# First route: all rows kept in SBUF, normalised by ScalarE in the scaling rounds and the selection

## The reference, cut to what matters

```
x = x + 0.5 * ffn(layernorm(x)); x = x + mixer(layernorm(x)); x = x + 0.5 * ffn(layernorm(x))

def ffn(x):                                   # x is normalised
    logits = x @ gate_w                       # (8, 2048, 8 experts)
    t = log(clip(logits, 1e-6))
    for _ in range(8):                        # Sinkhorn: over the tokens, then over the experts
        t = t - logsumexp(t, tokens); t = t - logsumexp(t, experts)
    vals, idx = top_k(exp(t) per expert, 256) # 256 tokens for each expert
    routed_back[idx] = (x[idx] @ experts[e]) * vals     # where experts share a token, the last stands
```

## Time and profile before

| | us |
|---|---|
| median of 3 runs (lowest, highest) | 3546.92 (3545.2, 3549.64) |
| the profiled execution | 3556.01 |
| its span, first to last instruction | 3554.5 |

### The profile page before, as it was taken

How to read it: one execution, slowest core, us unless ns; L and a number is a source line. 1 busy time by engine, 2 the same in 40 slices (tenths; PEclk the granted TensorE clock), 3 DMA queues, 4 the chain that set the end, 5 groups by cost and what they waited for, 6 DMA issues and landing times. The chain is left out here.

```text
span 3554.5 us, 29882 instructions
## 1 busy us (share of the span) xinstructions
PE 2753.7 (77%) x9684; PEld 1514.2 (43%) x9684; DVE 3150.0 (89%) x2664; ACT 2099.4 (59%) x2219; POOL 1295.2 (36%) x871
## 2 busy tenths in 40 slices
PE   6303778899889889988988998898789677874555
PEld 4202333354346335434634543463345255433444
DVE  7996489999999999999999999999999968994555
ACT  6101568876877787687778768677866634221111
POOL 0003254437244443724444372444011110016665
PEclk8556899999899999989999998999899887885777
DMA  8103377788778778877877887787677669233342
GB/s 332 66 0 108 84 171 177 153 180 182 154 172 164 177 153 179 183 153 172 163 177 155 180 183 151 173 163 174 127 145 139 130 122 364 89 158 117 131 143 89
DMA packets 128024, 553.85 MB, mean 156 GB/s; under 512 B 19782, under 2 KB 55272, under 8 KB 79424
## 3 DMA queue, kind: packets, MB, share of 16 engines
q0 software_dynamic: 75168, 393.49, 53.1%
q1 hardware_dynamic: 52736, 158.94, 12.1%
HBM read 152.62 MB, written 117.45 MB: 76 GB/s over the span
## 5 line engine op out<-in xcount | busy, mean ns | idle before, releaser
L1312 DVE TENSOR_TENSOR_SCAN state<-state,drive 128x2048 f32<-128x2048 f32 x512 | 2223.7, 4404 | 51.0 <-ACT state L1518 50.9
L1518 ACT ACTIVATE state<-delta,neg_a 128x2048 f32<-128x2048 f32 x512 | 1018.8, 2005 | 216.8 <-DMA delta<-xc 84.0
L1769 PE MATMUL ps_states<-state,ident 128*128 128x512 f32 x1792 | 854.3, 622 | 78.7 <-DMA state<-state 64.3
L1193 POOL DMA_DIRECT2D state<-state x255 | 233.5, 916 | 1310.1 <-DVE state L1312 1286.4
L1671 PE MATMUL ps_proj<-x1t,w_in 128*128 128x512 f32 x1024 | 514.5, 648 | 84.7 <-ACT xc L1467 29.8
L1769 PEld LDWEIGHTS ps_states<-state,ident 128*128 128x128 f32 x1792 | 349.1, 201 | 482.0 <-issue 384.8
L1687 PE MATMUL ps_proj<-conv_in,tap 128*128 128x512 f32 x1024 | 488.7, 629 | 54.5 <-ACT conv_in L1431 33.9
L1122 POOL DMA_INDIRECT picked<-normed_rows,slot_now x112 | 353.5, 3157 | 100.5 <-PE ps_rows L1652 55.7
L1671 PEld LDWEIGHTS ps_proj<-x1t,w_in 128*128 128x128 f32 x1024 | 207.2, 207 | 369.2 <-issue 281.3
L1138 POOL DMA_INDIRECT x<-routed_rows,row_now x112 | 339.2, 3029 | 34.6 <-issue 34.6
L1687 PEld LDWEIGHTS ps_proj<-conv_in,tap 128*128 128x128 f32 x1024 | 204.3, 202 | 320.6 <-issue 280.8
(11 more groups left out here) (344 smaller groups left out, 3288.4 us busy)
## 6 DMA issues: line engine op xcount, KB each, us to landing
state<-state POOLq DMA_DIRECT2D x255, 1024.0 KB
delta<-xc POOLq DMA_DIRECT2D x24, 1024.0 KB
normed_rows<-rows_in SPq DMA_DIRECT2D x8, 2048.0 KB
x_rows<-x SPq DMA_DIRECT2D x16, 1024.0 KB
dense_rows<-dense_mid SPq DMA_DIRECT2D x16, 1024.0 KB
f_dense<-dense_rows SPq DMA_DIRECT2D x16, 1024.0 KB
rows_in<-in_x SPq DMA_DIRECT2D x7, 2048.0 KB
expert<-in_experts SPq DMA_DIRECT2D x56, 256.0 KB
```

What stands on the lines that cost most here:

```text
L1193: nc.gpsimd.dma_start(out=state[held(q)][:], in_=state[held(q - 1)][:], accum_op=ALU.add).then_inc(pair_landed(b, q // 2)[0], 16)
L1312: nc.vector.tensor_tensor_scan(state[held(q)][:], state[held(q)][:], drive[j % 2][:], 0.0, ALU.mult, ALU.add).then_inc(state_ready, 1)
L1518: nc.scalar.activation(state[held(q)][:], delta[j % 2][:], ACT.Exp, scale=g.neg_a[:, j, n:n + 1]).then_inc(decay_ready, 1)
L1769: mm = nc.tensor.matmul(ps_sum[c][:], g.ident[:], state[held(q)][:, c * CH:(c + 1) * CH], start=(opening and n == 1), stop=(n == N - 1))
```

## The change: what it does, and the diff

In the first route the stage has eight row buffers instead of four, one for each batch. They and the per-batch reciprocals and shifts belong to `route` now (`KeptRows`), so that they live through both blocks. SP issues all eight batches' loads at the start, ahead of the weights, and no load waits for a store. Nothing is normalised in the load phase. ScalarE normalises batches 0 to 2 after it has copied the last logits, and batches 3 to 7 at the start of its stream in the selection block. SP stores batches 0 to 2 at the end of its stream in the gates stage, batches 3 to 7 in the selection block, at whose end it waits for all eight stores. The second route keeps its four buffers and its loads; its semaphore `shift_done` counts by 3 for each batch instead of 2.

```diff
+class KeptRows:
+    FIRST = 3
+    def __init__(self, nc, out, ctx):
...
+        self.rows = sb("kept_rows", [P, T, D])
+        self.rstd, self.shift = sb("kept_rstd", [P, T]), sb("kept_shift", [P, T])
...
+def normalise_rows(nc, k, b):
+    for t in range(T):
+        nc.scalar.activation(k.rows[b][:, t, :], k.rows[b][:, t, :], ACT.Identity, bias=k.shift[b][:, t:t + 1],
+                             scale=k.rstd[b][:, t:t + 1]).then_inc(k.normed, 1)
+
+def store_rows(sp, k, b):
+    sp.wait_ge(k.normed, (b + 1) * T)
+    sp.dma_start(k.out[b], k.rows[b][:]).then_inc(k.stored, 16)
...
-    U = 4
+    U = NB if kept else 4
...
-    rows_ = [sb(f"rows{u}", [P, T, D]) for u in range(U)]
+    rows_ = kept.rows if kept else [sb(f"rows{u}", [P, T, D]) for u in range(U)]
...
     @block.sync (gates stage)
-        for b in range(NB):
-            if last:
-                if b + U < NB:
...
-            sp.wait_ge(normed_act, act_normed(b + 1))
-            sp.wait_ge(normed_dve, min(b + 1, NB - 1) * ON_DVE)
-            sp.dma_start(xn_out[b], rows_[b % U][:]).then_inc(row_out[b % U], 16)
-            if b >= 1 and b - 1 + U < NB:
-                sp.wait_ge(row_out[(b - 1) % U], ((b - 1) // U + 1) * 16)
-                sp.dma_start(rows_[(b - 1) % U][:], x_in[b - 1 + U]).then_inc(row_in[(b - 1) % U], 16)
+        for b in range(NB - U):
+            sp.wait_ge(stats_done, (b + 1) * T)
+            sp.wait_ge(turns_done, (b + 1) * G2)
+            sp.dma_start(rows_[b % U][:], x_in[b + U]).then_inc(row_in[b % U], 16)
...
-        for u in range(U):
-            sp.wait_ge(row_out[u], 16 * NB // U)
+        for b in range(kept.FIRST):
+            store_rows(sp, kept, b)
         sp.wait_ge(g.loaded, 5 * 16)
...
     @block.vector (gates stage)
-            nc.vector.reciprocal(rstd[b % 2][:], std[b % 2][:]).then_inc(rstd_done, 1)
-            dve.wait_ge(rstd_done, b + 1)
-            nc.vector.scalar_tensor_tensor(shift[b % 2][:], means[b % 2][:], -0.5, rstd[b % 2][:],
+            nc.vector.reciprocal(kept.rstd[b][:], std[b % 2][:]).then_inc(shift_done, 1)
+            dve.wait_ge(shift_done, 3 * b + 1)
+            nc.vector.scalar_tensor_tensor(kept.shift[b][:], means[b % 2][:], -0.5, kept.rstd[b][:],
...
-                if b and t >= T - ON_DVE and not last:
-                    normalise(b - 1, t)
...
-                dve.wait_ge(*((std_done, b - 1) if last else (normed_act, act_normed(b - 1))))
+                dve.wait_ge(std_done, b - 1)
...
     @block.scalar (gates stage)
-                if b and i >= Q and not last:
-                    for t in range((i - Q) * 2, (i - Q + 1) * 2):
-                        normalise(b - 1, t)
...
-        for t in () if last else on_act(NB - 1):
-            normalise(NB - 1, t)
+        for b in range(kept.FIRST if kept else 0):
+            act.wait_ge(shift_done, 3 * (b + 1))
+            act.wait_ge(turns_done, (b + 1) * G2)
+            normalise_rows(nc, kept, b)
...
     @block.sync (selection)
+        for b in range(kept.FIRST, NB) if kept else ():
+            store_rows(sp, kept, b)
+        if kept:
+            sp.wait_ge(kept.stored, NB * 16)
...
     @block.scalar (selection)
+        for b in range(kept.FIRST, NB) if kept else ():
+            normalise_rows(nc, kept, b)
```

More of the change, by code:

```diff
@@ L128, in _, with sb @@
             nc.scalar.mul(flat, flat, -1.0)
+class KeptRows:
+    FIRST = 3
+    def __init__(self, nc, out, ctx):
+        def sb(name, shape):
+            return [ctx.enter_context(nc.sbuf_tensor(f"{name}{b}", shape, F32)) for b in range(NB)]
+        self.out = out
+        self.rows = sb("kept_rows", [P, T, D])
+        self.rstd, self.shift = sb("kept_rstd", [P, T]), sb("kept_shift", [P, T])
+        self.normed, self.stored = nc.alloc_semaphore("kept_normed"), nc.alloc_semaphore("kept_stored")
+def normalise_rows(nc, k, b):
[5 more added lines that the diff above has]
+    sp.dma_start(k.out[b], k.rows[b][:]).then_inc(k.stored, 16)
 def route(nc, g, x, tag, last=None):
@@ L137, in route, with gates_stage @@
         rows = ctx.enter_context(nc.sbuf_tensor(f"gate_rows_{tag}", [P, NT // 2], F32))
+        k = None if last else KeptRows(nc, xn_out, ctx)
         with ExitStack() as c1:
-            gates_stage(nc, g, x_in, xn_out, rows, tag, last, c1)
+            gates_stage(nc, g, x_in, k, rows, tag, last, c1)
         with ExitStack() as c1:
-            top_stage(nc, g, rows, tag, last, c1)
+            top_stage(nc, g, k, rows, tag, last, c1)
         nc.clear_and_free_semaphores(nc.allocated_since(held))
         nc.all_engine_barrier()
-def gates_stage(nc, g, x_in, xn_out, rows, tag, last, ctx):
+def gates_stage(nc, g, x_in, kept, rows, tag, last, ctx):
     def sb(name, shape, dt=F32):
@@ L164, in gates_stage @@
     GROUPS = NB * G2 // Q
-    ON_DVE = 8
-    rows_ = [sb(f"rows{u}", [P, T, D]) for u in range(U)]
+    rows_ = kept.rows if kept else [sb(f"rows{u}", [P, T, D]) for u in range(U)]
     stats = [sb(f"stats{u}", [P, T, 6]) for u in range(2)]
@@ L169, in gates_stage @@
     std = [sb(f"std{u}", [P, T]) for u in range(2)]
-    rstd = [sb(f"rstd{u}", [P, T]) for u in range(2)]
-    shift = [sb(f"shift{u}", [P, T]) for u in range(2)]
     scale = sb("row_scale", [P, 2, Q, 2, H, HB])
@@ L182, in gates_stage @@
     row_in = [sem(f"row_in{u}") for u in range(U)]
-    row_out = [sem(f"row_out{u}") for u in range(U)]
     probs = sb("probs", [P, 2, Q, 2, H, HB, E])
@@ L201, in gates_stage @@
                                                      "sum_spread", "expert_scale_done", "token_scaled"))
[L202 to L207, removed]
+    eps_set, summed, wide_set, stats_done, moments_done, std_done, shift_done = (
+        sem(n) for n in ("eps_set", "gate_summed", "wide_gate_set", "stats_done", "moments_done", "std_done", "shift_done"))
+    turns_done, turned_copied, logits_done, rows_copied, logits_turned, scaled = (
+        sem(n) for n in ("turns_done", "turned_copied", "logits_done", "logit_rows_copied", "logits_turned", "logits_scaled"))
     block = ctx.enter_context(nc.Block())
@@ L216, in landed @@
         return (first_in[t // TP], 16) if b == 0 else (row_in[b % U], (b // U + (b % U > 0)) * 16)
[L218 to L224, removed]
     def of_tokens(tile, h):
@@ L288, in scales @@
             dve.wait_ge(std_done, b + 1)
+            to_scale = scale[:, :, :, :, b // HB, b % HB]
             if last:
-                nc.vector.reciprocal(scale[:, :, :, :, b // HB, b % HB],
-                                     std[b % 2][:].rearrange("p (k q o) -> p o q k", k=2, o=2)).then_inc(shift_done, 2)
+                nc.vector.reciprocal(to_scale, std[b % 2][:].rearrange("p (k q o) -> p o q k", k=2, o=2)).then_inc(shift_done, 3)
                 return
-            nc.vector.reciprocal(rstd[b % 2][:], std[b % 2][:]).then_inc(rstd_done, 1)
-            dve.wait_ge(rstd_done, b + 1)
-            nc.vector.scalar_tensor_tensor(shift[b % 2][:], means[b % 2][:], -0.5, rstd[b % 2][:],
+            nc.vector.reciprocal(kept.rstd[b][:], std[b % 2][:]).then_inc(shift_done, 1)
+            dve.wait_ge(shift_done, 3 * b + 1)
+            nc.vector.scalar_tensor_tensor(kept.shift[b][:], means[b % 2][:], -0.5, kept.rstd[b][:],
                                            ALU.mult, ALU.mult).then_inc(shift_done, 1)
[L297 to L305, removed]
+            nc.vector.tensor_copy(to_scale, kept.rstd[b][:].rearrange("p (k q o) -> p o q k", k=2, o=2)).then_inc(shift_done, 1)
         nc.vector.memset(eps[:], LN_EPS).then_inc(eps_set, 1)
@@ L344, in _ @@
         scales(NB - 1)
-        dve.wait_ge(shift_done, 2 * NB)
+        dve.wait_ge(shift_done, 3 * NB)
         for o in range(2):
@@ L416, in deviation @@
             nc.scalar.activation(std[b % 2][:], spread[b % 2][:], ACT.Sqrt, bias=eps[:, 0:1], scale=1.0 / D).then_inc(std_done, 1)
[L418 to L423, removed]
         act.wait_ge(eps_set, 1)
@@ L517, in _, with top_stage @@
                                 gates[:, t % 2, t // 2].rearrange("p k h b e -> p (k h b e)"), g.ident[:]).then_inc(rows_turned, 1)
-def top_stage(nc, g, rows, tag, last, ctx):
+def top_stage(nc, g, kept, rows, tag, last, ctx):
     def sb(name, shape, dt=F32):
```

4 lines of the change are left out of this document (removed).

## The result

The changed kernel took 3511.52 us (median of 7 runs, 3507.17 to 3522.34), beside 3546.55 us for the kernel before on the same chip (7 runs, 3533.03 to 3549.64): a ratio of 0.991, 95% interval 0.9893 to 0.9928. In microseconds that is 35.0 less by the medians and 25 to 38 by the interval, which holds the 30.7 of the forecast. The profiled execution took 3512.88 us, with a span of 3511.2.

What follows compares the result with a forecast made beforehand. The load phase was taken as bound by VectorE while four buffers last, then by loads waiting for stores. 58.61 - 1.42 + 2.03 = 59.22 us against 89.89, nothing lost later: 3546.9 - 30.7 = 3516.2 us, range 3510 to 3526.

Steps and rivals of the forecast that it cites:

- The load phase: First route, first statistics to first multiply with the logits: 59.22 us against 89.89, so the rounds begin 30.67 us earlier.
- (a): Load phase: take the second route's phase, 58.61 us, which holds VectorE's own pace of 6.20 us per batch.
- (b): Load phase: the first route's second batch starts 9.02 us after the first, against 10.44 in the second route: -1.42 us.
- (c): Load phase: three small scale operations per batch stay, 0.46 us against 0.17, seven times between statistics: +2.03 us.
- Cost 0: Scaling rounds and selection: ScalarE's moved passes add nothing; upper bounds 0.4 us in the rounds, 1.3 us in the selection.
- cover: Rounds: ScalarE idles 36.18 us before its gate-row copies; 32 added passes take 15.9 us, leaving 20 us.
- The sum: Whole kernel: median of the kernel before, 3546.9 us, less 30.7 us gives 3516.2 us.
- The last term of the sum: Barriers, mixer and second route follow as before; the three runs of the kernel before lie within 4.4 us.
- The 9.1 us: Whole kernel before: profiled execution lay 9.1 us over the runs' median of 3546.92; no row placed it, difference kept.
- Rival 1: Load phase: TensorE becomes the bound because its clock falls; 3530 us, chance 0.06.
- Rival 2: Load phase: seven queued loads land together, second batch later than 47.5 us; 3551 to 3559, say 3555 us; chance 0.03.
- Rival 3: Rounds and selection slow beside moved passes and stores, giving back 23 to 31 us; 3540 to 3548, say 3544; chance 0.03.

Runs made afterwards that it cites:

- The two experiments of the first group: Kernel before with eight row buffers in the first route and nothing else: 3538.02 us; kernel before with four buffers and first-route normalising left out: 3538.66 us.
- The experiments with eight and six batches: Changed kernel with eight, or six, batches normalised before ScalarE's gate-row copies instead of three: 3529.36 and 3519.44 us.
- the first group: Runs on one chip, including both kernels unedited (before 3551.97 us, changed 3518.48 us) and each half of the change alone.
- third execution: Changed kernel run once more without edits, on another chip than its first repeat: 3508.32 us, ratio 0.9894 to the kernel before.
- the second and third group: Runs of the changed kernel and its edited variants on another chip; the kernel before took 3550.4 and 3545.69 us there.
- first repeat: Changed kernel run again without edits: 3518.48 us, ratio 0.9895 to the kernel before.

## Why the prediction was right, point by point

**The load phase.** 59.33 us against a forecast of 59.22, so its three terms hold in sum. (a) VectorE's pace is the phase's: 6.53 us per batch, forecast 6.49. (b) The second batch starts 16.90 - 7.96 = 8.94 us after the first, forecast 9.02. (c) The three small operations take 20.80 - 20.34 = 0.46 us, as in the earlier trace rows. The two experiments of the first group show that neither the late loads nor VectorE's passes alone would have been the whole of it.

That the forecast came within 0.11 us is in part luck. Over eleven executions in which the second route's loads are not edited, its phase takes 56.90 to 58.69 us. Nearly all of that scatter is the landing of the second batch, whose statistics begin 9.00 to 10.54 us after the first ones; the way from there to the multiply is 47.74 to 48.17 us. The correction (b) took just this landing out of the sum, and what was left of (a) is the part that repeats.

**The rounds and the selection.** Cost 0 was right: 44.51 and 149.70 us, to the digit those of before. The 48 passes took 23.71 us (forecast 23.9), the 80 took 39.44 (39.8), and 20.44 us of cover were left (20). The experiments with eight and six batches show that this cover is a real limit: had the diff moved all 128 passes ahead of the gate rows, 18.6 of the 30.4 us would have been lost.

**The sum.** 3516.2 against a measured 3511.52. The mechanism was right. The forecast allowed for a gain of 30.67 us, and 30.40 came in the first route. The medians of the two unedited kernels differ by 35.0 us in the first result, 34.8 in the first group and 37.4 in the third, with intervals of 25 to 38, 28 to 46 and 31 to 44 us. Two of these hold the forecast gain and the third just does not. The last term of the sum, that everything behind the first route repeats, may thus be short by some microseconds, but that is not clear of the scatter. The 9.1 us by which the profiled execution lay over its median were rightly left alone: in the repeat the profiled execution took 3550.79 us beside a median of 3551.97.

Between the two profiled executions lie 43.3 us of span, 12.9 of them behind the first route: 3.2 in the opening of the mixer, 1.7 in the second route's load phase (58.61 and 56.90 us), 6.5 in the last layer. Here are the windows of two stretches, the opening of the mixer up to the first scan, and the last layer from its last MAX8 to the last start of an f_finished. The kernel before, then its repeat:

```profile
367.70:408.85 41.15, 35.37 (x80) 15.81 (x80) 5.85 (x11) 20.33 (x23) 2.83 (x3) 0.85 0.11 30
3155.80:3519.90 364.10, 194.05 (x990) 149.71 (x991) 217.22 (x655) 55.38 (x113) 214.63 (x206) 0.71 0.37 128
```

```profile
368.50:408.20 39.70, 33.87 (x80) 15.36 (x80) 5.87 (x10) 20.33 (x23) 2.83 (x3) 0.88 0.11 33
3150.50:3514.50 364.00, 184.80 (x990) 143.54 (x991) 217.13 (x655) 55.43 (x113) 213.77 (x206) 0.72 0.38 128
```

The changed kernel, and its third execution:

```profile
336.20:374.15 37.95, 32.14 (x80) 14.62 (x80) 5.88 (x10) 20.36 (x23) 2.85 (x3) 0.94 0.12 35
3119.40:3477.00 357.60, 190.77 (x989) 148.01 (x990) 217.42 (x655) 55.12 (x113) 214.61 (x206) 0.73 0.39 131
```

```profile
335.50:376.70 41.20, 35.41 (x80) 15.82 (x80) 5.88 (x10) 20.35 (x23) 2.85 (x3) 0.85 0.11 31
3123.10:3477.70 354.60, 191.30 (x990) 147.37 (x991) 217.36 (x654) 55.30 (x113) 216.11 (x206) 0.71 0.38 132
```

The opening goes by its granted clock: 41.15 us at 0.85, 37.95 at 0.94, and the changed kernel too has 41.20 at 0.85 in another execution. It is scatter of 3 us, not an effect of the change.

The last-layer stretch is another matter: 361.9 to 366.9 us in the four kernels that have the code of before (the two half changes among them), 354.6 to 357.8 in eight of the changed code and its variants, and 363.1 in one, its first repeat. The means are 364.2 and 357.4. VectorE, ScalarE and GpSimd are busy as long in both, so it is waiting that differs, and VectorE and ScalarE wait much for gathers there (65.9 to 131.6 us for either engine in the four windows of the first pair and its repeats).

It does not go by the time at which the stretch begins: the kernel that normalises everything in the gates stage starts its mixer at 280.6 us and has 356.3, the one with eight buffers alone starts it at 278.9 and has 361.9. But it may go by the chip. On the chip of the first group the changed kernel's 363.1 lies among the 361.9, 364.0 and 366.9 of the others; the seven of the second and third group, 354.6 to 357.8, ran on another chip, and there no execution of the kernel before was profiled. Only the first pair, 364.1 and 357.6, remains, and on which chip each of the two was profiled is not known. The diff changes only the counting of a semaphore in the second route, which lies before this stretch. Whether the change shortens this stretch at all stays open.

**The rivals.** Rival 1 did not come: the clock of the phase was 0.98, and it stayed at the upper level even with an eighth of the products between the transposes. Rival 2 neither: the second batch began at 16.90, not past 47.5, and the weights ahead of it showed that loads land in turn. Rival 3 came to nothing; its break-even is 17%, 30.7 of the 182.7 us that VectorE is busy in the two stages, where the prediction took some 170 us and 18%.

## What to carry to other kernels

When a program holds the same loop a second time without the work that you want to move away, its phase is the best estimate there is: its time, corrected by the few rows that differ, came within 0.2 us. Look then at the queue as well as at the engines: where loads stand behind stores for want of buffers, freeing VectorE alone left a phase of 79.10 us with the DMAs busy all through it. And ask of every moved instruction which idle stretch of its engine it goes into and how long that is; here an idle stretch of 36 us took 16 us of passes for nothing, and with all 128 in it the first route lost 18.6.

## What the runs showed of the hardware that was not expected

- SP's issue of one load with many small pieces (conv_w) held the engine for 21.01 us behind seven queued batch loads; in the kernel before it took 4.97 us, behind three. In the changed kernel nothing waited for SP. With eight buffers alone something did: it took 20.81 us there, and the first store, issued at 27.47 us in the kernel before, was issued at 46.95 although its batch was normalised by about 27 us.
- The rise of the granted clock in the mixer's opening came about 13 and 10 us into its window in two executions of the kernel before, about 5 us in two of the changed one and 13 in its third, at the cost of some 3 us between them.
- A microsecond saved at the second batch was worth a fifth to a third of one at the phase's end. The loads and the deviations that ScalarE makes come close behind VectorE, which the busy times of the window (51.48 us for VectorE, 50.53 for TensorE, 37.49 for ScalarE, of 59.33) do not tell.
